# Merged attention of a decoder program: gathers of two batches as plain rows, operand copies part by part, and a new order of VectorE's work

## The chip, the cores and the metric

The program runs on one NeuronCore of a Trainium2 chip. The metric is device time in microseconds (us), from the start of the one launch to its end; lower is better.

## The reference, cut to what matters

The program is a decoder of two layers over 8 batches of 512 tokens, 256 features, in float32. The change touches one stage, `mix_heads`, which finishes the first layer and computes the first two thirds of the second:

```python
# end of layer 0: four expert rows are added to each token
y = y.at[tok].add(out)
# layer 1, a recurrence over time with one decay for each feature, then a 256x256 product
h = h * A + x_t ;  out = einsum('sbd,do->bso', hs, BC)
# layer 1, attention of 16 heads of 16 features: values, keys from the context, queries from x
energy = einsum('nqhd,nkhd->nhqk', q, k) ;  masked where mask == 0
attention = softmax(energy / sqrt(256), axis=3)
out = einsum('nhql,nlhd->nqhd', attention, v) @ Wo.T + bo
# each result is added to x, and each input is layernorm(x)
```

## The kernel before, in words

The tensor `x` lies in SBUF (128 partitions, 32 tiles of 256 features; a batch is 4 tiles). Ahead of this stage the experts' rows were written to DRAM, and `place` holds for each token the numbers of its four rows. A batch passes through three jobs in `mix_heads`:

1. **Gather.** GpSimd issues 16 indirect DMAs (4 tiles, 4 rows of each token), which read rows of `outputs` and add them in flight to `x` (`gathers`, L905). VectorE then takes the statistics (`gathered_sums`, L1292), a chain of tiny operations makes mean and variance (L1305 to L1315), ScalarE the root (L1210), VectorE the reciprocal (`root_of`, L1321).
2. **Recurrence** (`combine`): VectorE normalizes (`rec_norm`, L1329), TensorE transposes (item `rtp`, L1070), VectorE scans (L1337), TensorE multiplies (item `rout`, L1076), VectorE adds to `x` (L1341), then statistics and the chain again (`added_sums`, `norm_all`).
3. **Attention.** Five `prep` items: context transposed (0), normalized x transposed (1), keys (2), queries (3), values (4). Keys and queries are split into three bf16 parts so that bf16 matmuls keep float32's precision: ScalarE writes part 0 (L1166), VectorE the residue (`residue`, L1251), ScalarE part 1 (L1174), GpSimd part 2 (`third_part`, L912). SP stores each part to DRAM (`store_part`, L839) and copies the parts back as stacks, six copies of keys and six of queries for each of the four head groups (`stacks`, L846). On the stacks TensorE computes the energies twice: queries by keys in PSUM `wide` (`first_energies`, L1008), whose row maxima VectorE takes (`maxima`, L1256); and keys by queries in PSUM `slim` with the negated maxima as extra rows (`second_energies`, L1019), which ScalarE turns into `prob` (L1190). The maxima get there through GpSimd (`split_max`, L927 to L933), a TensorE transpose (`rows`, L1039), a VectorE copy (L1262) and a GpSimd DMA (`max_rows`, L939). `values` (L1031) multiplies `prob` with the values; ScalarE copies the result out, TensorE transposes it (`turn`, L1046), VectorE divides (L1269, L1272). Three `fin` items apply the output matrix (L1055, L1061), and VectorE adds to `x` (L1281).

The work is written out by hand, in place of a scheduler. A batch is 4 groups (g) of 8 steps (n); each step is two tiles of second energies and one item of first energies, the latter 12 steps ahead of their use. Tables say at which (g, n) other items stand: `PREP_AT`, `REST_AT` (residue), `PART1_AT`, `FIN_AT`, `REC_AT`, `NORM_AT`, `ADDED_AT`, `SUMS_AT`, `CHAIN_AT`, `ROOT_AT`, `TURN_AT` = 4, `ROWS_AT` = 5. In batch b the attention of b runs, with the preps of b+1, the end of b-1, the recurrence of b+2 and the gather of b+3. The list `BEFORE` is what runs ahead of batch 0: batches 0 and 1 are gathered and mixed there, and batch 0 prepared.

All items of `wide` share two PSUM buffers in turn: an item on TensorE waits until the item two before it in the list of TensorE's order has been read out (`wide_freed`). `slim` has three buffers. Every engine runs its own list strictly in order.

## Time and profile before

| | |
|---|---|
| time, median of 3 runs | 2812.26 us (2808.93 to 2823.7) |
| the profiled execution | 2824.53 us; its span 2822.8 us, 1.7 us lie around it |
| `mix_heads` in the span | from 1061 to about 1785 us |
| batches 1 to 4 in it | about 79 us each |

The profiled execution is 12.3 us above the median and 0.8 us above the slowest of the three runs. Times in the trace count from the span's start. In a row, "[x <-engine tile line]" is the engine's idle time just before the instruction and what ended it; PEld is TensorE's weight load, SPq and POOLq are queues.

### The profile page before, as it was taken

The numbers are of one execution on the slowest core, as the hardware profiler recorded it, in microseconds if no ns is written. First come the engines' busy times: TensorE is split into PE (matmuls) and PEld (weight loads), VectorE is DVE, ScalarE is ACT, GpSimd is POOL, SyncE is SP. The second block draws the span as 40 slices with busy tenths as digits, with TensorE's granted clock in tenths as the row PEclk, the third lists the DMA queues.
The fourth block names the chain that finished last, engine by engine and source line by source line (L and its number), as shares of the span: only waits on it lengthen the run. The fifth ranks groups of instructions, "written<-read, shape, count | busy, mean of one in ns | idle before, by whom it ended". The sixth has DMA issues, their size and how long they took to land. (4 is left out here: it accounts for less than half of the span.)

```text
span 2822.8 us, 40193 instructions
## 1 busy us (share of the span) xinstructions
PE 2320.4 (82%) x12094; PEld 1621.0 (57%) x12095; DVE 1255.2 (44%) x2608; ACT 830.4 (29%) x1871; POOL 884.9 (31%) x1110
## 2 busy tenths in 40 slices
PE   4888685455599983578888889699989999999998
PEld 2444573223377772223333333365569999999997
DVE  4444215552144442567767767258712222222222
ACT  1111110111044441255556666322211221221221
POOL 1000000047600007455535311022225445455443
PEclk9999765778699995689999999899999999999999
DMA  8300110063355546444434310220017777777775
GB/s 282 133 0 0 34 41 16 0 247 116 111 156 156 157 146 101 96 104 98 105 96 99 77 60 27 85 97 30 16 59 236 243 255 237 245 253 236 244 254 161
DMA packets 203554, 360.75 MB, mean 128 GB/s; under 512 B 29302, under 2 KB 182367, under 8 KB 195272
## 3 DMA queue, kind: packets, MB, share of 16 engines
q1 hardware_dynamic: 160456, 299.94, 31.1%
q0 software_dynamic: 43008, 59.70, 10.8%
q8 instruction: 46, 0.75, 0.1%
q14 instruction: 44, 0.36, 0.0%
HBM read 261.83 MB, written 97.13 MB: 127 GB/s over the span
## 5 line engine op out<-in xcount | busy, mean ns | idle before, releaser
L2449 PE MATMUL me_hp<-me_xgT,me_w 128*128 128x160 f32 x3072 | 440.7, 301 | 0.6 <-DVE me_xgT L2491 0.6
L2449 PEld LDWEIGHTS me_hp<-me_xgT,me_w 128*128 128x128 f32 x3072 | 425.1, 191 | 1.5 <-DVE me_xgT L2491 0.7
L1256 DVE TENSOR_REDUCE hd_nmax<-hd_wide 128x2 f32<-128x1024 f32 x256 | 307.8, 1219 | 120.1 <-PE hd_wide L1008 119.5
L1190 ACT ACTIVATE hd_prob<-hd_slim 128x512 f32<-128x512 f32 x512 | 276.3, 601 | 202.6 <-PE hd_slim L1019 201.8
L2505 DVE TENSOR_TENSOR me_hid<-me_act_out,me_hp 128x160 f32<-128x160 f32 x384 | 123.4, 321 | 372.0 <-ACT me_act_out L2477 372.0
L2458 PE MATMUL me_op<-me_hid,me_w 128*128 128x160 f32 x1536 | 236.0, 304 | 0.0
L1019 PE MATMUL hd_slim<-hd_q_stack,hd_k_stack 100*128 100x512 bf16 x512 | 199.0, 392 | 38.9 <-ACT hd_prob L1190 27.5
L1008 PE MATMUL hd_wide<-hd_k_stack,hd_q_stack 97*128 97x512 bf16 x512 | 201.4, 398 | 26.4 <-DVE hd_rest L1251 14.9
L2477 ACT ACTIVATE me_act_out<-me_hp 128x160 f32<-128x160 f32 x384 | 116.4, 303 | 347.6 <-PE me_hp L2449 347.6
L2458 PEld LDWEIGHTS me_op<-me_hid,me_w 128*128 128x128 f32 x1536 | 213.8, 190 | 2.6
L905 POOL DMA_INDIRECT all_x<-outputs,rt_place x128 | 200.6, 1568 | 42.0 <-issue 36.5
L2149 PE MATMUL me_r_hp<-me_r_xnT,me_r_sw 128*128 128x512 f32 x384 | 169.1, 597 | 0.0
L1881 PE MATMUL mr_e_hp<-mr_w,mr_e_xtT 128*128 x640 | 167.7, 385 | 0.8 <-issue 0.8
L1019 PEld LDWEIGHTS hd_slim<-hd_q_stack,hd_k_stack 100*128 100x128 bf16 x512 | 50.0, 99 | 196.3 <-ACT hd_prob L1190 81.2
L1031 PE MATMUL hd_pv<-hd_prob,hd_v 128*32 128x512 f32 x1024 | 139.2, 616 | 3.9 <-ACT hd_oT L1154 3.6
L1733 POOL DMA_INDIRECT places<-mr_s_xn,mr_s_now x128 | 124.6, 974 | 55.2 <-issue 33.2
L2107 POOL TENSOR_TENSOR me_r_hid<-me_r_act_out,me_r_up_out 128x512 f32<-128x512 f32 x48 | 64.4, 1342 | 217.5 <-ACT me_r_up_out L2205 217.5
L2395 POOL DMA_INDIRECT out_x<-me_oa,me_then_a x64 | 104.0, 1625 | 69.5 <-issue 35.8
L2149 PEld LDWEIGHTS me_r_hp<-me_r_xnT,me_r_sw 128*128 128x128 f32 x384 | 73.1, 192 | 85.4 <-issue 85.0
L1937 DVE TENSOR_TENSOR mr_e_hid<-mr_e_act_out,mr_e_hp 128x128 f32<-128x128 f32 x160 | 46.2, 289 | 165.0 <-ACT mr_e_act_out L1913 165.0
L1881 PEld LDWEIGHTS mr_e_hp<-mr_w,mr_e_xtT 128*128 128x128 f32 x640 | 110.3, 193 | 10.4 <-issue 1.6
L2479 ACT ACTIVATE me_oT<-me_op 128x320 f32<-128x320 f32 x64 | 28.0, 437 | 242.1 <-PE me_op L2458 242.1
(373 smaller groups left out, 3674.3 us busy)
## 6 DMA issues: line engine op xcount, KB each, us to landing
me_w<-in_L_ffn_w_exp SPq DMA_DIRECT2D x64, 2304.0 KB, 9.0
places<-z_zero SPq DMA_DIRECT2D x23, 1008.0 KB, 11.0
mr_e_xt<-places SPq DMA_DIRECT2D x160, 144.0 KB, 2.2
outputs<-mr_e_y SPq DMA_DIRECT2D x160, 128.0 KB, 1.7
part_rows<-hd_parts SPq DMA_DIRECT2D x48, 256.0 KB, 2.3
hd_k_stack<-part_rows SPq DMA_DIRECT2D x192, 64.0 KB, 2.4
hd_q_stack<-part_rows SPq DMA_DIRECT2D x192, 64.0 KB, 2.7
mr_w<-in_L_ffn_w_in SPq DMA_DIRECT2D x4, 2048.0 KB, 18.3
```

The lines of the kernel that those rows point to most:

```text
L905: nc.gpsimd.indirect_dma_start(out=x[:, r * TB + j, :], out_offset=None, in_=outputs[:, :], in_offset=bass.IndirectOffsetOnAxis(ap=place[: ...
L1008: last = nc.tensor.matmul(wide[:, at, j, :], q_stack[0:FIRST_ROWS, bt.slot, h, qc * P:(qc + 1) * P], k_stack[0:FIRST_ROWS, bt.slot, h, :], ...
L1019: nc.tensor.matmul(slim[:, slim_slot(bt, item), :], k_stack[:, bt.slot, h, kc * P:(kc + 1) * P], q_stack[:, bt.slot, h, :], start=True, st ...
L1031: last = nc.tensor.matmul(pv[32 * j:32 * j + 32, :], v[:, slot, kc, head(g, j), :], prob[:, kc * GH + j, :], start=(kc == 0), stop=(kc == ...
L1190: nc.scalar.activation(prob[:, u, :], slim[:, slim_slot(bt, item), :], ACT.Exp, scale=D ** -0.5)\
L1256: nc.vector.tensor_reduce(nmax[:, g % 2, n // 2, c:c + 2], wide[:, at], AX.X, ALU.max, negate=True)\
L1733: nc.gpsimd.indirect_dma_start(out=places[:, :], out_offset=bass.IndirectOffsetOnAxis(ap=now[:, j, n:n + 1], axis=0), in_=xn[:, j, :], in_ ...
L1881: last = nc.tensor.matmul(hp[:, v, 0:2 * F], xtT[:, v, c, :], w1[:, bass.ds(e, 1), c, :].rearrange("p a n -> p (a n)"), start=(c == 0), st ...
L2149: last = nc.tensor.matmul(hp[:, u % 2, half, :], sw1[:, c, at:at + P], xnT[:, c, b * S:(b + 1) * S], start=(c == 0), stop=(c == DC - 1))
L2449: last = nc.tensor.matmul(hp[:, f % 3, half * CAP:(half + 1) * CAP], w1[:, sl, c, cols], xgT[:, sl, c, :], start=(c == 0), stop=(c == DC - 1))
L2458: last = nc.tensor.matmul(op[:, c, 0:CAP], w2[:, sl, f, c * P:(c + 1) * P], hid[:, sl, f, :], start=(f == 0), stop=(f == FC - 1))
L2505: nc.vector.tensor_tensor(hid[:, sl, f, :], act_out[:, f % 2, :], hp[:, f % 3, 0:CAP], ALU.mult).then_inc(h_free, 1)
```

## The change

- **Plain gathers for batches 0 and 1.** The 32 indirect DMAs (`gathered_rows`) write rows into tiles of `prob`, which is not yet in use, tile by tile, and add nothing; VectorE adds the four rows and x (`add_rows`: per tile four additions of 128x256 and the statistics). The second batch's gathers move ahead of GpSimd's `third_part(0, 0)`. Three memsets go from GpSimd to VectorE.
- **The list before batch 0.** The recurrence of batch 1 moves behind the first eight energies; `rows(0,0,0)` moves behind its transposes.
- **Stacks part by part.** SP copies all key stacks as soon as the key parts are stored, then the queries' copies of parts 0 and 1, then those of part 2.
- **Split by half.** ScalarE's part 0 and VectorE's residue work on two halves of 512 columns.
- **The tables.** Item `prep` 1 moves from step 1 to 3, `prep` 3 from 4 to 6, the queries' residue from (0,5) to (0,7); GpSimd's part 2 of the queries and the bias move one group later; the recurrence moves two to six steps later, the sums of gathered rows one step, the root of the variance into ScalarE's step (3,7) and VectorE's next batch.
- **VectorE's order in a step.** `turn` stands ahead of the maximum of its step, `rows` right behind it; `normed` stands behind the maximum of step 2 and no longer ahead of the batch.

```diff
-        PREP_AT = (0, 1, 2, 4, 6)
-        REST_AT, PART1_AT = (3, 5), (4, 6)
+        PREP_AT = {0: 0, 2: 2, 3: 1, 4: 4, 6: 3}
+        REST_AT, PART1_AT = ((0, 3), (0, 7)), ((0, 4), (1, 0))
...
-        REC_AT = {(1, 3): ("rtp", 2, 0), (1, 5): ("rtp", 2, 1), (1, 7): ("rout", 2, 0), (2, 3): ("rout", 2, 1)}
-        NORM_AT, ADDED_AT = ((1, 0), (1, 2)), ((2, 0), (2, 5))
-        SUMS_AT, CHAIN_AT, ROOT_AT = ((3, 3), (3, 4)), ((3, 5), (3, 6)), (3, 6)
+        REC_AT = {(1, 5): ("rtp", 2, 0), (1, 7): ("rtp", 2, 1), (2, 3): ("rout", 2, 0), (2, 5): ("rout", 2, 1)}
+        NORM_AT, ADDED_AT = ((1, 1), (1, 3)), ((2, 6), (2, 7))
+        SUMS_AT, CHAIN_AT, ROOT_AT = ((3, 4), (3, 5)), ((3, 6), (3, 7)), (3, 7)
+        ROOTED_AT, NORMED_AT, THIRD_AT = 1, 2, (0, 6)
 
         BEFORE = [("prep", 0, n) for n in (0, 2, 4)] + [("rtp", 0, 0), ("rtp", 0, 1), ("rout", 0, 0), ("rout", 0, 1)]\
-            + [("prep", 0, n) for n in (1, 3)] + [("rtp", 1, 0), ("rtp", 1, 1), ("rout", 1, 0), ("rout", 1, 1)]\
-            + [("energy", 0, n // NSTEP, n % NSTEP) for n in range(NSTEP + LEAD)]
+            + [("prep", 0, n) for n in (1, 3)] + [("energy", 0, 0, n) for n in range(NSTEP)]\
+            + [("rtp", 1, 0), ("rtp", 1, 1), ("rout", 1, 0), ("rout", 1, 1)] + [("energy", 0, 1, n) for n in range(LEAD)]
...
-                    for a in range(2):
-                        sp.wait_ge(part0_ready, b * 2 + a + 1)
-                        store_part(a, 0)
-                        sp.wait_ge(part1_ready, b * 2 + a + 1)
-                        store_part(a, 1)
-                        sp.wait_ge(part2_ready, b * 2 + a + 1)
-                        store_part(a, 2)
-                    sp.wait_ge(stored, (b + 1) * 6 * 16)
+                    for part in range(3):
+                        part_stored(b, 0, part)
+                    sp.wait_ge(stored, b * 96 + 48)
                     for g in range(NG):
-                        stacks(b, g)
+                        stacks(b, g, 0, range(NPAIR))
+                    for part in range(2):
+                        part_stored(b, 1, part)
+                    sp.wait_ge(stored, b * 96 + 80)
+                    stacks(b, 0, 1, range(NPAIR - 1))
+                    part_stored(b, 1, 2)
+                    for g in range(1, NG):
+                        stacks(b, g, 1, range(NPAIR - 1))
+                    sp.wait_ge(stored, b * 96 + 96)
+                    for g in range(NG):
+                        stacks(b, g, 1, range(NPAIR - 1, NPAIR))
...
+                def gathered_rows(r):
+
+                    for j in range(TB):
+                        wait(pool, gathered[j], r * TOP * 16)
+                        for n in range(TOP):
+                            nc.gpsimd.indirect_dma_start(out=row(r, j, n), out_offset=None, in_=outputs[:, :],
+                                                         in_offset=bass.IndirectOffsetOnAxis(ap=place[:, r * TB + j, n:n + 1], axis=0))\
+                                .then_inc(gathered[j], 16)
...
-                gathers(0, 0, ALL)
+                gathered_rows(0)
+                pool.wait_ge(zeroed, 3)
+                pool.wait_ge(ones_loaded, 32)
+                pool.wait_ge(mask_stored, 16)
+                pool.sem_inc(passed, 1)
+                gathered_rows(1)
                 pool.wait_ge(loaded, 8 * 16)
                 third_part(0, 0)
-                gathers(1, 0, ALL)
                 third_part(0, 1)
...
-                        if g == 0 and b < B - 1:
-                            third_part(b + 1, 0)
-                            third_part(b + 1, 1)
-                        if g == 1 and b < B - 1:
+                        if g < 2 and b < B - 1:
+                            third_part(b + 1, g)
+                        if g == NG - 1 and b < B - 1:
                             add_bias(b + 1)
                         if bt.gathers and g < NG - 1:
-                            gathers(b + 3, (0, 4, 10)[g], (4, 10, ALL)[g])
+                            gathers(b + 3, (0, 5, 10)[g], (5, 10, ALL)[g])
...
+                    for c in range(DC):
+                        dve.wait_ge(part0_ready, (b * 2 + a) * DC + c + 1)
+                        nc.vector.tensor_tensor(rest[:, a, c, :], wide[:, at, c, :], parts[:, a, 0, c, :], ALU.subtract)\
+                            .then_inc(rest_ready, 1)
...
+                def add_rows(r):
+
+                    for j in range(TB):
+                        t, at = r * TB + j, (r * TB + j) * TOP
+                        dve.wait_ge(gathered[j], (r + 1) * (16 * TOP))
+                        for n in (0, 2):
+                            nc.vector.tensor_tensor(row(r, j, n), row(r, j, n), row(r, j, n + 1), ALU.add).then_inc(taken, 1)
+                        dve.wait_ge(taken, at + 2)
+                        nc.vector.tensor_tensor(row(r, j, 0), row(r, j, 0), row(r, j, 2), ALU.add).then_inc(taken, 1)
+                        dve.wait_ge(taken, at + 3)
+                        nc.vector.tensor_tensor(x[:, t, :], x[:, t, :], row(r, j, 0), ALU.add).then_inc(taken, 1)
+                        dve.wait_ge(taken, at + 4)
+                        sums(t, 1)
...
                         for n in range(NSTEP):
+                            if n == TURN_AT and not (bt.first and g == 0):
+                                item = ("turn", 0, g)
+                                turn(bt.b * NG + g, bt.slot if g else 1 - bt.slot, (g - 1) % NG, slim_use(bt, item), slim_slot(bt, item))
                             item = ahead(g, n)
                             if not (bt.last and item[1]):
                                 maxima(item[2], item[3], wide_use(bt, item), wide_slot(bt, item))
```

**Place 1: VectorE ahead of batch 0.** The list of VectorE from the first normalization for attention (L1236, and L1262 after) on. Before:

```order
L1251 TENSOR_TENSOR hd_rest<-hd_wide,hd_parts 128x1024
L1292 BN_STATS all_stats<-all_x 128x6 x4
...
L1329 TENSOR_SCALAR hd_xn<-all_x,all_mean,all_rstd 128x256 x4
L1337 SCALAR_TENSOR_TENSOR hd_xT<-hd_decay,hd_wide 128x512 x2
L1341 TENSOR_TENSOR all_x<-all_x,hd_wide 128x512 x2
L1292 BN_STATS all_stats<-all_x 128x6 x4
...
L1256 TENSOR_REDUCE hd_nmax<-hd_wide 128x2 x12
L1262 COPY hd_nrows<-hd_slim 48x128
```

And with the change, from the same residue:

```order
L1280 TENSOR_TENSOR hd_rest<-hd_wide,hd_parts 128x512 x2
L1286 TENSOR_REDUCE hd_nmax<-hd_wide 128x2 x8
L1330 TENSOR_TENSOR hd_prob<-hd_prob 128x256 x2
L1332 TENSOR_TENSOR hd_prob<-hd_prob 128x256
L1334 TENSOR_TENSOR all_x<-all_x,hd_prob 128x256
L1322 BN_STATS all_stats<-all_x 128x6
...
L1381 SCALAR_TENSOR_TENSOR hd_xT<-hd_decay,hd_wide 128x512 x2
L1292 COPY hd_nrows<-hd_slim 48x128
L1385 TENSOR_TENSOR all_x<-all_x,hd_wide 128x512 x2
```

Eight maxima now stand between the queries' residue and all work on batch 1; four more come behind it.

**Place 2: VectorE in batch 6, groups 0 and 1.** Before, from the normalization for batch 7 (L1236) on; L1256 is a maximum, L1269 and L1272 the `turn`, L1281 the second item of `fin`:

```order
L1236 TENSOR_SCALAR hd_xn<-all_x,all_mean,all_rstd 128x256 x4
L1256 TENSOR_REDUCE hd_nmax<-hd_wide 128x2 x4
L1251 TENSOR_TENSOR hd_rest<-hd_wide,hd_parts 128x1024
L1256 TENSOR_REDUCE hd_nmax<-hd_wide 128x2
L1269 RECIPROCAL hd_rsum<-hd_slim 128x16
L1272 TENSOR_TENSOR hd_o<-hd_slim,hd_rsum 128x4x64
L1256 TENSOR_REDUCE hd_nmax<-hd_wide 128x2
L1251 TENSOR_TENSOR hd_rest<-hd_wide,hd_parts 128x1024
L1262 COPY hd_nrows<-hd_slim 48x128
L1256 TENSOR_REDUCE hd_nmax<-hd_wide 128x2 x7
L1269 RECIPROCAL hd_rsum<-hd_slim 128x16
L1272 TENSOR_TENSOR hd_o<-hd_slim,hd_rsum 128x4x64
```

With the change:

```order
L1286 TENSOR_REDUCE hd_nmax<-hd_wide 128x2
L1262 TENSOR_SCALAR hd_xn<-all_x,all_mean,all_rstd 128x256 x4
L1286 TENSOR_REDUCE hd_nmax<-hd_wide 128x2
L1280 TENSOR_TENSOR hd_rest<-hd_wide,hd_parts 128x512 x2
L1299 RECIPROCAL hd_rsum<-hd_slim 128x16
L1302 TENSOR_TENSOR hd_o<-hd_slim,hd_rsum 128x4x64
L1286 TENSOR_REDUCE hd_nmax<-hd_wide 128x2 x2
L1292 COPY hd_nrows<-hd_slim 48x128
L1286 TENSOR_REDUCE hd_nmax<-hd_wide 128x2 x2
L1280 TENSOR_TENSOR hd_rest<-hd_wide,hd_parts 128x512 x2
L1286 TENSOR_REDUCE hd_nmax<-hd_wide 128x2 x4
L1299 RECIPROCAL hd_rsum<-hd_slim 128x16
```

Five maxima stood ahead of group 0's `turn` and now four do; the fifth follows it.

**Place 3: TensorE at step 4 of group 1, with the change** (L1032 is a first energy, L1043 a second, L1085 the item of `fin`, L1070 the `turn`, L1063 the `rows`):

```order
L1032 MATMUL hd_wide<-hd_k_stack,hd_q_stack 128x512
L1085 MATMUL hd_wide<-hd_wo,hd_oT 128x256 x4
L1070 MATMUL hd_slim<-all_ident,hd_oT 128x128 x4
L1043 MATMUL hd_slim<-hd_q_stack,hd_k_stack 128x512
L1032 MATMUL hd_wide<-hd_k_stack,hd_q_stack 128x512
L1043 MATMUL hd_slim<-hd_q_stack,hd_k_stack 128x512
L1032 MATMUL hd_wide<-hd_k_stack,hd_q_stack 128x512
L1063 MATMUL hd_slim<-all_ident_bf,hd_nparts 128x128
```

This order is that of before, with other line numbers: on TensorE the `turn` still stands behind the `fin` or `prep` item of its step.

## Rows read from the trace of the kernel before

**Rows 1.** Windows: busy time of each engine, granted clock (1.00 is full), by stretch.
```profile
1061.00:1168.20 107.20, 41.06 (x114) 22.67 (x115) 46.74 (x93) 9.22 (x12) 72.95 (x58) 0.60 0.60 113
1261.60:1340.00 78.40, 67.84 (x364) 29.09 (x364) 56.19 (x80) 46.28 (x79) 39.04 (x46) 0.98 0.42 96
```
**Rows 2.** Waits of PE, from 1261.6 to 1735 us: total, times, longest.
```profile
PE hd_slim L1039 <- DVE hd_o L1272: 15.7, 13, 2.5
PE hd_wide L1008 <- DVE hd_rest L1251: 12.7, 12, 1.2
...
PE hd_wide L1070 <- DVE hd_xn L1329: 5.6, 5, 1.2
```
**Rows 3.** Timeline, start and duration: the gathers of batch 0 and their statistics.
```profile
1063.42 1.63 POOL L905 DMA_INDIRECT all_x<-outputs,rt_place  x1 [0.28 <-POOL hd_zero L897]
...
1077.45 1.55 POOL L905 DMA_INDIRECT all_x<-outputs,rt_place  x1 [3.90 <-DMA all_x<-outputs,rt_place]
...
1095.99 1.55 POOL L905 DMA_INDIRECT all_x<-outputs,rt_place  x1 [0.30 <-issue]
...
1099.94 0.75 DVE L1292 BATCH_NORM_STATS2 all_stats<-all_x 128x6 f32<-128x256 f32 x2 [2.96 <-DMA all_x<-outputs,rt_place]
```
**Rows 4.** Tiles and lines: issue of plain indirect DMAs, duration ns min/median/max.
```profile
L2009 POOL DMA_INDIRECT me_xa<-token_rows,me_now_a x64: 982/1051/1061, 2079.5 to 2776.6; - x64
L1733 POOL DMA_INDIRECT places<-mr_s_xn,mr_s_now x128: 967/971/1334, 583.6 to 761.0; - x128
```
**Rows 5.** Timeline: two additions of 128x128, then normalization and reciprocal round a recurrence.
```profile
1075.33 0.28 DVE L1242 TENSOR_TENSOR hd_wq<-hd_wq,hd_blocks 128x128 f32<-128x128 f32 x1
1075.54 0.28 DVE L1242 TENSOR_TENSOR hd_wv<-hd_wv,hd_blocks 128x128 f32<-128x128 f32 x1
...
1102.72 1.38 DVE L1329 TENSOR_SCALAR hd_xn<-all_x,all_mean,all_rstd 128x256 f32<-128x256 f32 x4
...
1117.33 0.18 DVE L1321 RECIPROCAL all_rstd<-hd_dev 128x4 f32<-128x4 f32 x1 [0.38 <-ACT hd_dev L1210]
```
**Rows 6.** Timeline: queries' residue, part 2, first stacks, maxima, and the first second energies.
```profile
1126.88 1.23 DVE L1251 TENSOR_TENSOR hd_rest<-hd_wide,hd_parts 128x1024 f32<-128x1024 f32 x1 [7.96 <-ACT hd_parts L1166]
...
1129.28 2.22 POOL L912 TENSOR_TENSOR hd_parts<-hd_rest,hd_parts 128x1024 bf16<-128x1024 f32 x1
...
1133.66 2.93 SPq L846 DMA_DIRECT2D hd_k_stack<-part_rows  x6
...
1136.63 2.81 SPq L846 DMA_DIRECT2D hd_q_stack<-part_rows  x6
...
1151.27 14.12 DVE L1256 TENSOR_REDUCE hd_nmax<-hd_wide 128x2 f32<-128x1024 f32 x12
...
1168.19 0.61 PE L1019 MATMUL hd_slim<-hd_q_stack,hd_k_stack 100*128 100x512 bf16 x1 [3.96 <-DMA hd_q_stack<-hd_nrows]
```
**Rows 7.** Timeline, batch 2, group 1, step 4: energies, output product, turn.
```profile
1372.20 1.89 PE L1061 MATMUL hd_wide<-hd_wo,hd_oT 128*128 128x256 f32 x8
1372.40 1.23 DVE L1256 TENSOR_REDUCE hd_nmax<-hd_wide 128x2 f32<-128x1024 f32 x1 [0.46 <-PE hd_wide L1008]
1373.93 0.60 PE L1046 MATMUL hd_slim<-all_ident,hd_oT 128*128 128x128 f32 x4
...
1374.57 0.26 DVE L1269 RECIPROCAL hd_rsum<-hd_slim 128x16 f32<-128x16 f32 x1 [0.94 <-PE hd_slim L1046]
1374.59 0.38 PE L1008 MATMUL hd_wide<-hd_k_stack,hd_q_stack 97*128 97x512 bf16 x1
...
1374.86 0.42 DVE L1272 TENSOR_TENSOR hd_o<-hd_slim,hd_rsum 128x256 f32<-128x256 f32 x1
```
**Rows 8.** Timeline, batch 2, group 0, steps 3 and 4: maximum, residue, next energy.
```profile
1349.21 1.22 DVE L1256 TENSOR_REDUCE hd_nmax<-hd_wide 128x2 f32<-128x1024 f32 x1 [1.37 <-PE hd_wide L1008]
...
1350.35 1.21 DVE L1251 TENSOR_TENSOR hd_rest<-hd_wide,hd_parts 128x1024 f32<-128x1024 f32 x1
...
1351.62 0.39 PE L1008 MATMUL hd_wide<-hd_k_stack,hd_q_stack 97*128 97x512 bf16 x1 [1.13 <-DVE hd_rest L1251]
```
**Rows 9.** Timeline, batch 2, group 3, steps 3 to 5: statistics, rows, copy of maxima.
```profile
1409.01 0.75 DVE L1292 BATCH_NORM_STATS2 all_stats<-all_x  x2 [1.93 <-DMA all_x<-outputs,rt_place]
...
1411.64 0.10 PEld L1039 LDWEIGHTS hd_slim<-all_ident_bf,hd_nparts 128*128 128x128 bf16 x1 [2.99 <-POOL hd_nparts L933]
...
1414.81 0.20 DVE L1262 COPY hd_nrows<-hd_slim 48x128 bf16<-48x128 bf16 x1
```
**Rows 10.** Timeline: one VectorE addition of 128x4 alone, and one beside GpSimd's part 2.
```profile
1100.73 0.17 DVE L1305 TENSOR_TENSOR all_mean<-all_stats 128x4 f32<-128x4 f32 x1
...
1201.97 4.79 POOL L912 TENSOR_TENSOR hd_parts<-hd_rest,hd_parts 128x1024 bf16<-128x1024 f32 x2
...
1205.67 1.12 DVE L1305 TENSOR_TENSOR all_mean<-all_stats 128x4 f32<-128x4 f32 x1
```

More of the change, by code:

```diff
@@ L1359, in batch @@
                                 maxima(item[2], item[3], wide_use(bt, item), wide_slot(bt, item))
-                            if g == 0 and n in REST_AT and nxt is not None:
-                                item = ("prep", 1, REST_AT.index(n) + 2)
-                                residue(nxt.b, REST_AT.index(n), wide_use(bt, item), wide_slot(bt, item))
-                            if n == TURN_AT and not (bt.first and g == 0):
-                                item = ("turn", 0, g)
-                                turn(bt.b * NG + g, bt.slot if g else 1 - bt.slot, (g - 1) % NG, slim_use(bt, item), slim_slot(bt, item))
                             if n == ROWS_AT and not (bt.last and g == NG - 1):
@@ L1387, in batch @@
                                     gathered_sums(r3, SUMS_AT.index((g, n)))
-                                many = 2 * TB if bt.gathers else TB
                                 if (g, n) == CHAIN_AT[0]:
@@ L1416, in _ @@
                     if item == ("rtp", 1, 0):
-                        for pair in range(2):
-                            gathered_sums(1, pair)
+                        add_rows(1)
                         norm_all(TB, TB, 12, 2)
```

73 lines of the change are left out of this document (41 added, 32 removed).

## The prediction

> **What bounds the kernel now.** I read the windows first. `mix_heads` has two parts that this change touches: an entry of 107.2 us in which TensorE is busy 41 us at a mean granted clock of 0.60, and batches of some 79 us in which it is busy 67.8 of 78.4 us at 0.98 [rows 1]. So the entry is a chain of dependent steps, and a batch is bound by TensorE plus what it waits for. Everything outside the stage is untouched and I take its time as it is.
>
> Then the waits of TensorE over batches 1 to 6 [rows 2]: for VectorE's `turn` (hd_o) 15.7 us in 13 waits, for its residue 12.7 us in 12, for its normalization 5.6 us in 5. All are of VectorE, which is busy 56 of 78 us: it is not full, but its order decides. Last the timeline of the places where something moves.
>
> **Entry, gathers.** GpSimd issues 16 accumulating gathers from 1063.42 to 1097.5 at a pitch of 1.55 + 0.30 us, with a 3.9 us wait for a landing among them; the last statistics end at 1100.7 [rows 3]. The trace shows no plain gather from `outputs`, but one from another tensor at 1.05 us and a plain scatter at 0.97 [rows 4]. I take 1.05 + 0.30 = 1.35 us, and the gathers start at about 1062.2 since the memsets are gone: 16 end at 1083.8, 32 at 1105.4. Now VectorE has to add. An addition of 128x128 has a pitch of 0.21 us and lasts 0.28 [rows 5]; one of 128x256 has 128 more elements at some 1 ns each, so 0.34 and 0.42. A tile has one addition at pitch, three that wait for the one before (0.42 + 0.03 each) and statistics of 0.37 (two in 0.75, [rows 3]): 2.0 us, four tiles 8.2 us. They start behind the keys' residue, at 1087.6, and end at 1095.8, 4.9 us earlier than 1100.7. The queries' residue, which ended at 1128.1 [rows 6], then ends at 1123 (5 us earlier, and a little more for the halves).
>
> **Entry, stacks.** Before, the parts of the queries took until 1131.5, their storing until 1133.7, and the 12 copies of group 0 a further 5.7 us; with 2.5 us to land the first energies could have started at 1141.9 [rows 6]: 13.8 us behind the residue. Now: part 1 at 1124, part 2 at 1126.2, copies of parts 0 and 1 of group 0 from 1126.5 to 1128.9, the store of part 2, then the 15 copies of the other groups at 0.47 us each (7.1 us), and only then the copies of part 2: issued at 1136.8, landed at 1139.3. The key copies (24, 11.4 us) run from 1110.5 to 1121.8, hidden. So the energies of group 0 start at 1139.4, and VectorE has idled for 16 us.
>
> **Entry, order.** Behind that start stand on VectorE eight maxima at 1.18 us (12 took 14.1 us, [rows 6]) = 9.4, `add_rows(1)` 8.2, the chain 2.0, normalization 1.4, then from the end of a normalization (1104.1) to the end of the next reciprocal (1117.5) 13.4 [rows 5], and four maxima 4.7. In all 39.1 us from 1140.1, to 1179.2. TensorE turns to the first second energies two maxima earlier, at about 1177.5; before that was 1168.2 [rows 6], 2.8 us behind the last maximum because the copy of the maxima and its DMA came last, a path that `rows(0,0,0)` now takes early. **Entry: +9 us**. The 16 us of idleness, once filled with batch 1's work, is where it comes from.
>
> **Batches, `turn` first.** At step 4 of group 1 TensorE ends the energy at 1372.2, does the output product until 1374.0, the turn until 1374.5, and starts step 5's energies at 1374.59, because VectorE took the maximum at 1372.40 and left the buffer free; VectorE then waited 0.94 us for the turn and used it until 1375.28 [rows 7]. With `turn` ahead, the maximum starts at 1375.3 and ends at 1376.5. Step 5's energy takes the buffer of step 4's (the item two before, with the product between) and so starts at 1376.55: 1.96 us late. The same holds at group 0, where `prep` 4 (16 matmuls, about 1.95 us) stands in the product's place. Group 0 in batches 1 to 6, group 1 in 1 to 7: 13 x 1.96 = **+25.5**. In groups 2 and 3 nothing stands between energy and turn, step 5 uses another buffer, and it costs nothing.
>
> At (2,5) the item `rout` now follows and takes the buffer of (2,4), whose maximum is behind the turn: TensorE arrives some 1.2 us early, in 6 batches: **+7**.
>
> **Batches, `prep` 1 at step 3.** Before, the energy of step 4 took the buffer of the keys' projection, and TensorE did `values` (1.06 us) between; it still waited 1.13 us for the residue, which came behind the maximum [rows 8]. Now `prep` 1 takes that buffer right behind step 3's energy: the wait grows by `values` and little else, 1.2 us in 7 batches: **+8.4**. Halving the residue gains nothing there, since it waits for VectorE's maximum, not for ScalarE.
>
> **Batches, what is saved.** Of the 15.7 us for `turn`, some 11 stand in group 3, where TensorE at the same moment waits for GpSimd's maxima (2.99 us, [rows 9]); that wait is GpSimd's six gathers, which stay. The other 4.7 go. The queries' residue no longer stands between step 5's maximum and the next: of 6 waits of about 1 us, some 0.7 each, 4 us. The 5.6 us for normalization go, as it gets an earlier place. In group 3 the copy of the maxima came 3.2 us behind `rows` since VectorE waited for the gathered rows [rows 9]; one step later they are there and the copy comes at once, which lets GpSimd start 0.6 us sooner: 3 us in five batches. `prep` 1, the reciprocal and the normalization leave steps 0 and 1: about 0.65 us in 6 batches, 4 us. Sum **-21.3**. Stacks for later batches were ready well ahead and stay so: part 2 of the queries comes at (1,5), its copies land some 14 us later, and seven steps of 2 us and three inserted items lie before their use at (2,4). That cover is some 5 us; without it TensorE would wait for stacks.
>
> **Sum.** 9 + 25.5 + 7 + 8.4 - 21.3 = +28.6. Against the profiled execution of 2824.5: 2853.1. That execution is 12.3 us above the median, so 2841 for the median, 1.0% slower. The measurement can tell about 0.5%, 14 us, from no change.
>
> **A rule weighed.** A VectorE addition of 128x4 takes 0.17 us alone and took 1.12 us beside GpSimd's part 2, ending when that ended [rows 10]. `add_rows` is 16 such two-input additions in each batch, the first lot beside gathers being issued. If these held up each other for the 0.3 us of an addition, 16 of them would put `third_part(0,0)` 5 us later; the key copies would end at 1127 and the first energies start some 3 us later. The Trainium skill (SBUF — State Buffer, the section on the engine side's ports) says that VectorE with two SBUF inputs and a GpSimd operation that reads SBUF take one port pair as an exclusive lock; by that rule, the trace agrees. In the trace the gathers kept 1.55 us whatever VectorE did, so I give the sum nothing for it.
>
> **Rivals.**
> *The order pays (faster).* TensorE's waits on VectorE in a batch are 8 us of its 78 (the four groups took 21.2, 21.8, 15.1 and 20.3 us). If the maximum of step 4 is not what holds step 5, because TensorE gets there later than in rows 7, the +25.5 vanishes; if half of the 8 us went, that is -27 in 6.5 batches, with the entry 2824.5 - 18, for the median 2794. For it: VectorE's waits are many and small. Against: rows 7 have the three times beside each other. It decides at 0.5 us: under that at step 5 of groups 0 and 1, this rival holds. Chance 0.18.
> *Entry late, batches even.* Losses by `turn` and gains at the batch boundary balance: +9, 2821 for the median. For it: a step later elsewhere may hide half of each loss. Chance 0.20.
> *GpSimd is the late one.* If a plain gather costs the 1.86 us of an accumulating one, 32 end at 1121.7 and part 2 of the keys at 1124; key copies until 1138, the queries' until 1153, so the first energies come 14 us later, plus the blocking above, 3: +46, 2858. Against: two plain forms at 1.05 and 0.97 [rows 4]. Chance 0.09.
> *The forecast*, 0.53, with its own range 2826 to 2855: it takes 1.3 to 2.3 us for each late maximum and 5 to 12 us for the entry.
>
> **Numbers.** 2841. The range leaves out half of the first rival and some of the third: 2797 to 2862. Faster by over 0.5% (under 2798) 0.18, within 0.20, slower (over 2826) 0.62.
>
> **What would show it.** The first second energies near 1177; VectorE idle for 16 us before the first maximum; plain gathers near 1.05 us. In batches 1 to 6 a TensorE wait of about 2 us for the maximum at step 5 of groups 0 and 1, and one of over 2 us for the residue ahead of `prep` 1; the waits for hd_o nearly gone; a batch of 81 to 83 us. I am wrong if TensorE reaches step 5 late anyway, if the first energies start much before 1139, or if `rows` in group 3 no longer waits for GpSimd.

## The result, and the profile after

The changed kernel takes 2875.5 us (median of 4 runs, 2866.2 to 2880.2), the kernel before 2815.0 (4 runs): the ratio is 1.0208, 95% interval 1.0169 to 1.0248. That is 60 us at the median. Between the two profiled executions, both of which start the stage near 1061 us, it is 55.7 us (spans 2878.5 and 2822.8): 59.3 us within the stage, less 4.1 behind its last `rows` (1057.4 us before, 1053.3 after). Forecast were 2841 us and a range up to 2862: the sign was right, the size about half.

The windows of the kernel after, first the entry and two batches, then everything between the first `rows` (L1063) at step 5 of batch 0 and the last of batch 7. The columns, as in [rows 1], are the length, the busy time and instructions of TensorE, its weight load, VectorE, ScalarE and GpSimd, the granted clock, the share of the DMA engines and GB/s:

```profile
1061.62:1178.47 116.85, 39.85 (x114) 22.41 (x114) 55.97 (x125) 9.34 (x14) 53.40 (x55) 0.59 0.41 104
1299.30:1384.57 85.27, 71.28 (x365) 30.47 (x364) 57.09 (x82) 46.87 (x82) 39.18 (x46) 0.94 0.39 88
1475.57:1560.92 85.35, 71.16 (x366) 30.03 (x364) 56.19 (x82) 46.95 (x82) 39.11 (x46) 0.94 0.39 88
1197.68:1825.19 627.51, 509.82 (x2624) 209.42 (x2622) 408.44 (x573) 341.24 (x597) 238.52 (x310) 0.93 0.33 76
```

and the last of these for the kernel before:

```profile
1183.99:1765.38 581.39, 486.87 (x2635) 203.60 (x2634) 403.77 (x560) 339.36 (x584) 237.77 (x310) 0.97 0.35 83
```

These two long rows are the main reading. TensorE does the same work in both but for one item at the edge: in batch 0 the window after has the queries' projection (4 matmuls) where before it has that of the values (16), each about 2 us long. Yet it is busy 509.8 us against 486.9. So of the 46.1 us that the batches lost, 23.2 are idle time (117.7 against 94.5, the length less the busy time) and 22.9 are matmuls that took longer. The clock explains them. The stretches of the batches at the 1.2 GHz level, added up, are in the kernel before

```profile
sum 37.55, PE 21.10; mean PE 3.52
```

and after

```profile
sum 85.33, PE 66.83; mean PE 4.18
```

TensorE was busy for 21.1 us at the lower level before and for 66.8 after. Half of the difference is 22.9 us, and the busy time at the full clock plus half of that at the lower is 476.3 us before and 476.4 after. Each of the 16 stretches at the lower level after begins during a stop of TensorE of 1.2 to 3.2 us (the first: 19.5), or within 2 us of its end; not every such stop is followed by one. The forecast had 19.6 us for the batches, all of it waits.

The entry, as a timeline (this answers [rows 3, 6]):

```profile
1064.11 0.96 POOL L926 DMA_INDIRECT hd_prob<-outputs,rt_place  x1 [0.30 <-issue]
...
1139.14 1.44 PE L1032 MATMUL hd_wide<-hd_k_stack,hd_q_stack 97*128 97x512 bf16 x3 [19.82 <-issue]
...
1140.19 9.42 DVE L1286 TENSOR_REDUCE hd_nmax<-hd_wide 128x2 f32<-128x1024 f32 x8 [18.91 <-PE hd_wide L1032]
...
1178.47 0.63 PE L1043 MATMUL hd_slim<-hd_q_stack,hd_k_stack 100*128 100x512 bf16 x1
```

First energies at 1139.1 (forecast 1139.4), VectorE idle 18.9 us before its first maximum (forecast 16), first second energies at 1178.5 (forecast 1179 at the end of the maxima, 1177.5 for TensorE).

TensorE's waits in batches 1 to 6, which answer [rows 2] (total, times, longest):

```profile
PE hd_wide L1032 <- DVE hd_nmax L1286: 22.9, 14, 3.2
PE hd_wide L1011 <- DVE hd_rest L1280: 12.6, 5, 2.6
PE hd_wide L1100 <- DVE hd_nmax L1286: 7.6, 10, 1.1
...
PE hd_slim L1063 <- POOL hd_nparts L954: 4.9, 4, 1.2
```

The wait for hd_o is gone from the head of the list; the wait for a maximum has come. The timeline of the boundary from batch 3 to batch 4 (answers [rows 7, 8]) shows both at work:

```profile
1537.16 0.38 PE L1043 MATMUL hd_slim<-hd_q_stack,hd_k_stack 100*128 100x512 bf16 x1
...
1539.42 0.90 PE L1011 MATMUL hd_wide<-all_ident,hd_cx 128*128 128x128 f32 x3 [1.67 <-DVE hd_nmax L1286]
...
1541.18 0.63 PE L1043 MATMUL hd_slim<-hd_q_stack,hd_k_stack 100*128 100x512 bf16 x1
...
1551.39 1.09 PE L1011 MATMUL hd_wide<-all_ident,hd_xn 128*128 128x128 f32 x8 [2.51 <-DVE hd_rest L1280]
...
1558.64 0.42 DVE L1302 TENSOR_TENSOR hd_o<-hd_slim,hd_rsum 128x256 f32<-128x256 f32 x1
...
1558.98 1.21 DVE L1286 TENSOR_REDUCE hd_nmax<-hd_wide 128x2 f32<-128x1024 f32 x1
...
1560.25 0.39 PE L1032 MATMUL hd_wide<-hd_k_stack,hd_q_stack 97*128 97x512 bf16 x1 [1.72 <-DVE hd_nmax L1286]
```

`prep` 1 waits 2.51 us for the residue, and so at all its seven places (2.51 to 2.59; the first lies ahead of the first `rows` at step 5); step 5 waits 1.72 us for the maximum behind `turn`, at 13 places. And the same matmul of 512 columns lasts 0.38 us before TensorE has stood for 1.67 us at 1539.4 and 0.63 from about 1541 on: between the two, at 1538.8, the granted clock went from 2.4 to 1.2 GHz.

### The profile page after: what moved, and what is told of

Read it like the earlier page. It is cut to its first block and busy times, and to the rows that moved or that the text cites. A ratio compares the mean times of both kernels' runs of the same rounds, so it can differ in the third digit from the quotient of the medians.

```text
span 2878.5 us, 40278 instructions
## 1 busy us (share of the span) xinstructions
PE 2341.0 (81%) x12094; PEld 1623.9 (56%) x12095; DVE 1271.3 (44%) x2659; ACT 832.4 (29%) x1887; POOL 866.7 (30%) x1107
## 3 DMA queue, kind: packets, MB, share of 16 engines
q0 software_dynamic: 39936, 59.70, 10.1%
## 5 line engine op out<-in xcount | busy, mean ns | idle before, releaser
L1286 DVE TENSOR_REDUCE hd_nmax<-hd_wide 128x2 f32<-128x1024 f32 x256 | 305.4, 1217 | 116.9 <-PE hd_wide L1032 113.0
L1032 PE MATMUL hd_wide<-hd_k_stack,hd_q_stack 97*128 97x512 bf16 x512 | 205.1, 406 | 84.4 <-DVE hd_nmax L1286 32.0
L1043 PE MATMUL hd_slim<-hd_q_stack,hd_k_stack 100*128 100x512 bf16 x512 | 202.4, 398 | 8.7 <-DMA hd_q_stack<-hd_nrows 5.0
L917 POOL DMA_INDIRECT all_x<-outputs,rt_place x96 | 150.5, 1567 | 27.8 <-issue 27.6
L1055 PE MATMUL hd_pv<-hd_prob,hd_v 128*32 128x512 f32 x1024 | 146.8, 647 | 5.0 <-ACT hd_oT L1179 4.7
L1043 PEld LDWEIGHTS hd_slim<-hd_q_stack,hd_k_stack 100*128 100x128 bf16 x512 | 50.5, 100 | 172.3 <-issue 69.8
L1032 PEld LDWEIGHTS hd_wide<-hd_k_stack,hd_q_stack 97*128 97x128 bf16 x512 | 50.9, 101 | 151.2 <-DVE hd_nmax L1286 55.4
L1980 DVE TENSOR_TENSOR mr_e_hid<-mr_e_act_out,mr_e_hp 128x128 f32<-128x128 f32 x160 | 46.1, 288 | 165.2 <-ACT mr_e_act_out L1956 165.2
```

What stands on the lines that cost most here:

```text
L917: nc.gpsimd.indirect_dma_start(out=x[:, r * TB + j, :], out_offset=None, in_=outputs[:, :], in_offset=bass.IndirectOffsetOnAxis(ap=place[: ...
L1032: last = nc.tensor.matmul(wide[:, at, j, :], q_stack[0:FIRST_ROWS, bt.slot, h, qc * P:(qc + 1) * P], k_stack[0:FIRST_ROWS, bt.slot, h, :], ...
L1043: nc.tensor.matmul(slim[:, slim_slot(bt, item), :], k_stack[:, bt.slot, h, kc * P:(kc + 1) * P], q_stack[:, bt.slot, h, :], start=True, st ...
L1055: last = nc.tensor.matmul(pv[32 * j:32 * j + 32, :], v[:, slot, kc, head(g, j), :], prob[:, kc * GH + j, :], start=(kc == 0), stop=(kc == ...
L1286: nc.vector.tensor_reduce(nmax[:, g % 2, n // 2, c:c + 2], wide[:, at], AX.X, ALU.max, negate=True)\
```

## The experiments

All 18 kernels are compared by the stage's own marks, since the stage `mix_heads` starts at 1048 to 1064 us in one execution or another, with nothing changed ahead of it. "Entry" is from the start of the stage (its first memset, L887 or L905) to the first second energies, "batches" the stretch of the long rows above, "busy" and "idle" TensorE's within it, "stage" from the start of the stage to the last `rows`. The ratio is to the kernel before.

Each row but the ratio is one execution, and executions of the same code differ. e7 has the code of the kernel before in the batches, e6 that of e5: they agree within 1 us in busy time and within 2 in idle time. e4 has the code of the changed kernel there, and is busy 7.4 us less and idle 3.7 more. The entries of e6, e9, e10 and e11, again one code, spread over 1.6 us, e12 and e13 differ by 3.1, and e14 comes 3.8 behind the changed kernel. So steps from the changed kernel of less than some 8 us of busy time, and entries that differ by less than 4 us, show nothing by themselves.

| kernel | ratio (95%) | entry | batches | busy | idle | stage |
|---|---|---|---|---|---|---|
| before | | 107.1 | 581.4 | 486.9 | 94.5 | 704.3 |
| changed | 1.0208 (1.0169-1.0248) | 116.9 | 627.5 | 509.8 | 117.7 | 763.6 |
| e1_var | 1.0216 (1.0171-1.0261) | 116.9 | 630.7 | 513.8 | 116.9 | 766.8 |
| e2_turn | 1.0114 (1.0081-1.0148) | 117.1 | 595.5 | 500.3 | 95.2 | 731.5 |
| e3_prep1 | 1.0162 (1.0110-1.0215) | 117.0 | 615.9 | 500.3 | 115.6 | 749.0 |
| e4_entry | 1.0164 (1.0131-1.0197) | 104.4 | 623.8 | 502.4 | 121.4 | 746.7 |
| e5_turn_prep1 | 1.0070 (1.0045-1.0096) | 116.8 | 587.5 | 499.8 | 87.7 | 720.2 |
| e6_turn_prep1_entry | 1.0004 (0.9984-1.0024) | 104.3 | 587.5 | 500.2 | 87.3 | 707.5 |
| e7_plain | 0.9991 (0.9972-1.0011) | 108.2 | 580.6 | 487.9 | 92.7 | 704.3 |
| e8_turn_first | 1.0129 (1.0088-1.0169) | 107.0 | 609.3 | 500.3 | 109.0 | 732.3 |
| e9_bias | 0.9960 (0.9935-0.9985) | 105.0 | 580.4 | 493.4 | 87.1 | 701.0 |
| e10_root | 1.0021 (0.9998-1.0044) | 105.2 | 587.9 | 494.1 | 93.8 | 708.7 |
| e11_both | 0.9969 (0.9947-0.9992) | 103.6 | 575.5 | 488.0 | 87.4 | 694.9 |
| e12_prep | 0.9963 (0.9939-0.9987) | 102.1 | 576.1 | 491.3 | 84.7 | 693.6 |
| e13_third | 0.9955 (0.9936-0.9975) | 105.1 | 575.6 | 485.7 | 89.9 | 696.3 |
| e14_bias_changed | 1.0136 (1.0101-1.0170) | 120.6 | 617.5 | 505.7 | 111.7 | 757.3 |
| e15_bias_before | 1.0048 (1.0022-1.0073) | 107.8 | 592.8 | 493.7 | 99.1 | 716.1 |
| e16_stacks | 0.9935 (0.9911-0.9959) | 103.3 | 564.1 | 485.2 | 78.9 | 683.1 |

### e1: the variance a step earlier

```diff
-        ... CHAIN_AT, ROOT_AT = ((3, 4), (3, 5)), ((3, 6), (3, 7)), (3, 7)
+        ... CHAIN_AT, ROOT_AT = ((3, 4), (3, 5)), ((3, 5), (3, 6)), (3, 7)
```

> The changed kernel with one table entry different: VectorE ends the variance chain at steps (3,5) and (3,6) instead of (3,6) and (3,7), while ScalarE's root stays at (3,7). Theory A (ScalarE is held, and that is on the path): ScalarE's wait for hd_var, 13.2 us in 5 waits between 1299 and 1790 us, goes, the stretch from `rows` of group 3 to `rows` of group 0 gets 2 to 2.5 us shorter in six batches, and the span falls by 12 to 15 us from 2878.5 to about 2865. Theory B (it is hidden, because TensorE at that moment waits for VectorE's maximum anyway): 0 to 4 us, 2875 to 2878.

Nothing gained (stage +3.2, busy +4.0, idle -0.8). ScalarE's wait for hd_var over the batches only fell from 31.5 to 27.0 us, and behind it TensorE still stood for the residue. Theory A fell.

### e2, e3, e5: `turn` and `prep` 1 undone, alone and together

```diff
# e2: the four lines of maxima stand ahead of those of turn again
# e3:
-        PREP_AT = {0: 0, 2: 2, 3: 1, 4: 4, 6: 3}
+        PREP_AT = {0: 0, 1: 1, 2: 2, 4: 4, 6: 3}
-        ROOTED_AT, NORMED_AT, THIRD_AT = 1, 2, (0, 6)
+        ROOTED_AT, NORMED_AT, THIRD_AT = 0, 0, (0, 6)
```

> The changed kernel with VectorE's `turn` put back behind the maximum of its step; nothing else differs. Theory A (the forecast's term): the waits of 1.7 us at step 5 of groups 0 and 1 go, the span falls by 22 to 26 us to about 2854. Theory B (the order pays: something else is late at that place): 0 to 5 us. Theory C (each wait of TensorE also lowers its granted clock for a while): the fall is 30 to 35 us, to about 2846, and TensorE's busy time from `rows` of group 3 to `rows` of group 0 falls too.

> The changed kernel with `prep` 1 back at step 1, and the reciprocal and the normalization at step 0 behind its maximum (they stood ahead of it before the change). Theory A (the forecast's terms: +8.4 us for the move, -4 us for clearing steps 0 and 1): the span falls by 4 to 8 us, to about 2872. Theory C (the wait of 2.5 us ahead of `prep` 1 and the lower granted clock behind it are worth 4 us in each of seven batches): it falls by 20 to 28 us, to about 2854.

> The changed kernel with both edits of the two earlier runs undone: `turn` behind its maximum and `prep` 1 at step 1. Theory W (waits alone; each costs its own length): the stretch from `rows` of group 3 to `rows` of group 0, 26.0 us with `turn` undone alone, falls by the 2.5 us of the wait ahead of `prep` 1 to about 23.5, and the span to about 2828. Theory C (the waits also bring a stretch at half the granted clock, which goes only when they are all short): it falls to 21.5 to 22.5 us at a granted clock of 0.92 or more, and the span to 2814 to 2820.

e2: the stage is 32.1 us shorter; idle -22.5, as much as 13 waits of 1.72, and busy -9.6. That is Theory C by its size, though e4 is busy 7.4 us less with no such edit; the clean test of C is e8. e3 alone: -14.6, between A and C, of which 3.0 lie ahead of the batches; idle only -2.1 and busy -9.5. The 13 waits at step 5 stay at 1.72 us; the waits for the residue fall by 7.9 us, but 2.8 us come for ScalarE's copy of the context (hd_cT) and some 3 us elsewhere. With both undone the idle time falls by 7.5 against e2, near the forecast's 8.4 for `prep` 1. But the stretch from `rows` of group 3 to that of group 0 stayed at 24.5 to 25.2 us at a granted clock of 0.86 (27.4 at the loop's end): neither theory had it, something else was still late there.

### e4, e6, e7: the entry

```diff
-            + [("prep", 0, n) for n in (1, 3)] + [("energy", 0, 0, n) for n in range(NSTEP)]\
-            + [("rtp", 1, 0), ("rtp", 1, 1), ("rout", 1, 0), ("rout", 1, 1)] + [("energy", 0, 1, n) for n in range(LEAD)]
+            + [("prep", 0, n) for n in (1, 3)] + [("rtp", 1, 0), ("rtp", 1, 1), ("rout", 1, 0), ("rout", 1, 1)]\
+            + [("energy", 0, n // NSTEP, n % NSTEP) for n in range(NSTEP + LEAD)]
# e6: e5 with this, and rows(0, 0, 0) behind ("energy", 0, 1, 1)
# e7: the kernel before with gathered_rows and add_rows for batches 0 and 1 in place of gathers and sums
```

> The changed kernel with the list ahead of batch 0 in its old order (recurrence of batch 1, then twelve energies, then `rows`); gathers, additions and stacks stay as changed. Theory A (the forecast's term, the 16 us of idleness are filled again): the first energies still start at 1139 to 1140 us, the twelve maxima end near 1155 and the first second energies start at about 1157 to 1159, 20 us earlier than 1178.5; the span falls to about 2859. Theory B (the additions of batch 1 hold the queries' residue or the stacks, which come as late as what they save): the first second energies stay within 5 us of 1178.

> The kernel of the run before this one, and also the list ahead of batch 0 in its old order, with `rows` of group 0 two energies behind the eighth and not at the end of the list. The old order gave 11.4 us at the first second energies (1167.1 against 1178.5), which the earlier `rows` raise to 13 to 14, since the wait of 3.8 us for the maxima's copy goes: first second energies at 1164 to 1165. Theory W: span about 2814. Theory C: 2801 to 2807, faster than before by 0.5% or more.

> The kernel before with the plain gathers and the additions on VectorE for batches 0 and 1, and nothing else of the change. The forecast's term: the last statistics of batch 0 end 5 us earlier, so the first residue of the queries too; then the additions of batch 1 cost VectorE 6.7 us more than its statistics did, ahead of the twelve maxima. Theory A: gain and cost leave 2 to 5 us, span 2818 to 2821. Theory B (the additions of batch 1 stand on the path and the gain does not): slower by up to 3 us, 2823 to 2826.

The old order gave 12.5 us at the entry (104.4 against 116.9): the term of +9 holds. The 20 us that I expected did not come: VectorE is with batch 1's additions and recurrence until 1150.3, not until the first energies at 1139, and the twelve maxima (14.1 us) stand behind that. Of the 7.5 us that are missing 3 are `add_rows(1)`, which took 11.2 us and not 8.2 beside GpSimd's part 2 (last section). The earlier `rows` of e6 gave nothing to see: its maxima started 2.3 us later than those of e4 (89.9 and 87.6 us behind the stage's start), in code that is the same up to there, and the entry came out equal. Its span, 2822.1 us, is above both theories. e7 shows the plain gathers alone: entry +1.1, stage the same, ratio 0.9991, between A and B. They neither cost nor bring anything in the old order.

### e8: `turn` first, in the kernel before

> The kernel before with `turn` ahead of the maximum of its step, and nothing else of the change. Theory W (the forecast's term alone, 13 waits of 1.7 to 2 us, less the 4.7 us of waits for hd_o that go): 18 to 22 us slower, span about 2843. Theory C (with a lower granted clock behind the waits): 28 to 33 us slower, about 2854. Rival (the order pays or does nothing on the old tables): within 5 us of 2823.

The long row of this kernel:

```profile
1175.21:1784.54 609.33, 500.31 (x2635) 205.51 (x2634) 401.95 (x560) 341.87 (x584) 238.08 (x310) 0.94 0.34 79
```

Stage +28.0: idle +14.5, busy +13.4. Theory C, with one edit to the kernel before, whose busy time e7 repeats within 1.0. TensorE's waits for hd_o went altogether (18.6 us over the batches), and 11.9 us of waits for GpSimd's maxima came: the forecast's "some 11 stand in group 3" and stay. "The order pays" is dead.

### e9, e10, e11, e14, e15: GpSimd's bias and the root

```diff
# e9 (on e6), e14 (on the changed kernel)
-                        if g == NG - 1 and b < B - 1:
+                        if g == 1 and b < B - 1:
                             add_bias(b + 1)
# e10 (on e6): chain at (3, 5), (3, 6), root at (3, 6); e11: both
# e15: g == 1 made g == NG - 1 in the kernel before, nothing else
```

> The kernel with `turn`, `prep` 1 and the list ahead of batch 0 undone (batches 587.5 us from the first to the last `rows` of the eight batches, TensorE busy 500.2 and idle 87.3 of them; before 581.4, 486.9 and 94.5), and GpSimd's bias back from group 3 to group 1. Theory P (GpSimd's additions hold up VectorE's chain of tiny operations, 0.64 us each against 0.17, so the variance, the root and ScalarE's exponentials are late and the clock falls): the chain's operations take 0.17 to 0.20 us again, ScalarE's wait for hd_var shrinks from 2.3 to about 1 us, the stretch from `rows` of group 3 to that of group 0 falls from 24.5 to 22.5 us or less, batches 573 to 578 us. Theory R (the place of the root alone decides): the chain is quicker, but the stretch stays at 24 to 24.5 and the batches at 585 or more.

> The same kernel with the bias left in group 3, and instead the chain and the root one step earlier: (3,5), (3,6) and the root at (3,6), as before the change. Theory R: ScalarE is free for the exponentials of step 7 as before, the stretch from `rows` of group 3 to that of group 0 falls to 22.5 us or less, batches 573 to 578 us. Theory P: the chain now runs beside the bias all the same (or waits for it), the stretch stays at 23.5 to 24.5, batches 583 to 588 us.

> Both of the two edits before. Both theories: the stretch at 22 us or less with the granted clock at 0.92 to 1.00, TensorE busy about 487 us in the batches and idle about 85, batches 570 to 575 us, the first second energies 104.3 us behind the stage's start (before 107.1), so that the stage is 8 to 12 us shorter than before and the ratio 0.996 to 0.997. If the clock has a cause of its own that no wait explains, TensorE stays busy for 495 us or more.

> The changed kernel with nothing undone but GpSimd's bias, from group 3 back to group 1. Theory P (port): VectorE's chain at 0.17 us an operation, not 0.64; TensorE idle in the batches stays at 115 to 118 us, its busy time falls from 509.8 by 5 to 10 us, the span falls by 6 to 12 us to about 2869. Rival (hidden behind the wait ahead of `prep` 1): within 3 us of 2878.5.

> The kernel before with nothing changed but GpSimd's bias, from group 1 to group 3. Theory P: VectorE's chain of tiny operations at (3,5) takes 0.64 us each, ScalarE's root and the exponentials behind it come 1 to 2 us later, the stretch from `rows` of group 3 to that of group 0 grows from 22.3 to 23.5 to 24.5 us, batches 588 to 594 us instead of 581.4, the kernel 0.2 to 0.4% slower. Rival (VectorE and ScalarE have the time): batches within 2 us of 581.4.

The timeline of the kernel after, group 3 of batch 1: four additions of the bias, and VectorE's chain beside them:

```profile
1359.92 2.79 POOL L939 TENSOR_TENSOR all_x<-all_x,hd_bias 128x256 f32<-128x256 f32 x4
...
1361.43 0.64 DVE L1350 TENSOR_SCALAR all_mean<-all_mean  x1
...
1362.10 0.64 DVE L1351 TENSOR_TENSOR hd_half_diff<-all_stats 128x8 f32 x1
...
1364.81 0.21 ACT L1236 ACTIVATE hd_dev<-hd_var 128x8 f32<-128x8 f32 x1 [2.55 <-DVE hd_var L1359]
```

and of e9, the same operations without the bias beside them:

```profile
1406.98 0.17 DVE L1350 TENSOR_SCALAR all_mean<-all_mean  x1
...
1407.19 0.17 DVE L1351 TENSOR_TENSOR hd_half_diff<-all_stats 128x8 f32 x1
```

0.64 us against 0.17, and 0.64 is near the 0.70 us of one addition (2.79 for four). The Trainium skill (SBUF — State Buffer, the section on the two separate sides) has VectorE and GpSimd take one pair of ports as an exclusive lock, held for a whole instruction, when VectorE's instruction has two SBUF inputs and GpSimd's reads SBUF, or when VectorE's is in a two-port mode. By that rule, the trace agrees. The late variance holds ScalarE at the root (its waits for hd_var are 0.6 to 1.8 us in the batches of the kernel before and 1.1 to 3.2 in e15, but for one of 16.5 in batch 0 in both), its exponentials come late, and in e15 TensorE stands 4.6 us longer and its clock falls. e9: idle the same, busy -6.8 us, batches 580.4, a little above what P gave. e10 alone gained nothing (busy -6.1, idle +6.5; the chain mostly at 0.60 to 0.71 us again, R fell), both together (e11) brought busy to 488.0, as in the kernel before, and the batches to 575.5, near what both theories gave. e15, the bias alone moved in the kernel before, costs 11.4 us in the batches (busy +6.8, idle +4.6) and 0.48% in all: more than P expected. In e15:

```profile
1175.77:1768.57 592.80, 493.72 (x2636) 207.24 (x2634) 412.32 (x560) 339.44 (x584) 237.78 (x310) 0.95 0.35 81
...
1330.33 2.79 POOL L918 TENSOR_TENSOR all_x<-all_x,hd_bias 128x256 f32<-128x256 f32 x4
1330.43 0.68 DVE L1308 SCALAR_TENSOR_TENSOR hd_half_diff<-hd_half_diff 128x8 f32<-128x8 f32 x1
...
1333.39 0.21 ACT L1210 ACTIVATE hd_dev<-hd_var 128x8 f32<-128x8 f32 x1 [3.21 <-DVE hd_var L1315]
```

e14 takes the bias out of the changed kernel: batches -10.0 us (idle -6.0, busy -4.1). Here I had expected no change of the idle time. The ratio fell by 0.0072, about 20 us with some 15 either way.

### e12, e13, e16: the stacks

```diff
# e12 (on e11)
-        PREP_AT = {0: 0, 1: 1, 2: 2, 4: 4, 6: 3}
-        REST_AT, PART1_AT = ((0, 3), (0, 7)), ((0, 4), (1, 0))
+        PREP_AT = {0: 0, 1: 1, 2: 2, 4: 3, 6: 4}
+        REST_AT, PART1_AT = ((0, 3), (0, 5)), ((0, 4), (0, 6))
# e13 (on e12): third_part(b + 1, 0) and third_part(b + 1, 1) both at g == 0
# e16 (on e12)
                     part_stored(b, 1, 2)
-                    for g in range(1, NG):
-                        stacks(b, g, 1, range(NPAIR - 1))
                     sp.wait_ge(stored, b * 96 + 96)
-                    for g in range(NG):
-                        stacks(b, g, 1, range(NPAIR - 1, NPAIR))
+                    stacks(b, 0, 1, range(NPAIR - 1, NPAIR))
+                    for g in range(1, NG):
+                        stacks(b, g, 1, range(NPAIR))
```

> The kernel before this one and also the queries' projection back at step 4, its residue at (0,5) and part 1 at (0,6), as before the change. Theory S (the late stacks of the queries hold TensorE in group 2 of batch 0, 2.4 to 2.9 us and a clock dip): the stretch from `rows` of group 1 to that of group 2 in batch 0 falls from 21.9 to 17.6 to 18.5 us, the others change by less than 1 us. Rival (the stacks are in time either way, and the residue of the queries at (0,5) holds a maximum): no change there, and 0.5 to 1 us more from group 0 to group 1 in each batch, 3 to 6 us slower in all.

> The kernel of the run e12 (everything undone but gathers, stacks, halves and recurrence tables), with GpSimd's part 2 of the queries back right behind that of the keys in group 0. Theory T (the part is made a group late): the parts are stored 17 us earlier, the wait of 2.5 us for the stacks in group 2 of batch 0 goes, and the stretch from `rows` of group 1 to that of group 2 there falls from 21.5 to 17.6 to 18.2 us; batches 570 to 573 us. Rival: that stretch stays above 20 us, because the granted clock there has another reason.

> The kernel of the run e12, with part 2 of the queries left in group 1 of GpSimd, and only SP's order changed: the copies of part 2 for group 0 right behind its storing, ahead of the 15 copies of the other groups. Theory S (those 15 copies, 7 us, stand in the way): the copies for group 0 are issued by 1210.6 instead of about 1214 to 1216 on the scale of e12, the wait of 2.5 us goes or shrinks below 0.5, the stretch falls to 17.6 to 19 us; in the entry the first energies could start up to 7 us earlier but VectorE is busy with batch 1's recurrence, so nothing is gained there. Rival: part 2 itself is late, the wait stays above 2 us.

In e12 the stretch from group 1 to group 2 of batch 0 stayed at 21.5 us (17.6 before): S, as put there, fell (its rival's 3 to 6 us did not come either, the batches took 0.6 more than in e11). Its timeline says why, on SP's queue and TensorE:

```profile
1206.66 0.38 SPq L844 DMA_DIRECT2D part_rows<-hd_parts  x1
...
1207.08 8.97 SPq L859 DMA_DIRECT2D hd_q_stack<-part_rows  x19
...
1218.50 0.38 PE L1032 MATMUL hd_wide<-hd_k_stack,hd_q_stack 97*128 97x512 bf16 x1 [2.54 <-issue]
```

The store of part 2 was issued at 1206.7; of the 19 copies behind it (0.47 us each) the first 15 are those of the other groups, and the one of group 0, which is needed first, comes 16th, near 1214. e16 changes only this order, and Theory S holds: the wait is gone and that stretch becomes 17.5 us, the same stretch of batches 1 to 4 falls to 20.2 (20.3 to 23.5 in e12, 20.4 to 20.5 before), idle time by 5.8 and busy time by 6.1. e13 gets 18.9 us there by storing the part sooner, but 21.3 to 22.8 in batches 1 to 4, between its two theories; why was not followed up. e16 beats the kernel before and the changed one: 2797.2 us, ratio 0.9935 (0.9911 to 0.9959). Over the whole time it is not told apart from e12 (2799.6 us, 0.9963, the intervals overlap); its 12 us in the batches are one execution of each.

## Why the prediction was wrong, point by point

- **Entry +9: right, with some luck.** +9.8 at the first second energies, with plain gathers at 0.95 us (forecast 1.05), the idle VectorE and the eight maxima as forecast. That the first energies hit to 0.3 us is luck: the queries' residue ended at 1121.3 (forecast 1123), and the energies came 17.9 us behind it (forecast 16.4). Another 3.4 us came until the first `rows` at step 5, 2.5 of them the wait ahead of `prep` 1.
- **`turn` first +25.5: right, a little too large.** 13 waits of 1.72 us and not 1.96, 22.4 us; e2 gave 22.5 of idle time, e8 showed that some 12 of the hd_o waits come back as waits for GpSimd.
- **`rout` at (2,5) +7: too large.** The waits there were up to 1.1 us, and 8.2 us for both `rout` items over the batches against 4.3 before: 3.9 is new, since the item waited 0.4 us already.
- **`prep` 1 +8.4: right.** 2.51 against 1.13 us in seven batches is 9.7; e5 against e2 gave 7.5.
- **Saved -21.3: about 11 came out.** The idle time rose by 23.2 where the first three terms measured about 34.5 within the batches. The waits for hd_o and for the normalization did go, and the stretch from group 2 to group 3 became 1.0 us shorter. Part of what was not saved is at step 0: TensorE waits there 1.6 to 1.8 us for a maximum (1539.4 in the rows above), 8.6 us in all, and where the variance is earlier it waits 4.1 (e1) or 2.9 (e14). An estimate from single executions: the moved bias (idle 4.6 us in e15, 6.0 in e14) and the wait for stacks (2.4) account for 7 to 8 of the missing 10. That the idle time of the batches came near the forecast, 23.2 for 19.6, is therefore partly luck: the priced costs were too large by some 6 us, and two costs were left out.
- **The sum took each wait at its own length: the step that failed.** The batches' waits were forecast at +19.6 us and came to +23.2. But in [rows 1] a batch ran at 0.98, and I took the clock as given. After the longer stops the granted clock fell to the 1.2 GHz level and matmuls of 0.38 us took 0.63: 22.9 us, as much again as the waits (15.5 us in e4, with the same code in the batches). That added waits bring it is shown by single edits to the kernel before: e8 (idle +14.5, busy +13.4) and e15 (+4.6 and +6.8). Between the profiled executions the forecast was 27.1 us short (28.6 for 55.7): the clock is 22.9 of them, idle time in the batches 3.6, the entry up to the first `rows` at step 5 4.2 and the stage's start 0.5, less the 4.1 behind the stage.
- **Two edits that I priced at nothing.** GpSimd's bias in group 3, beside VectorE's chain (e9, e14, e15: 7 to 11 us). And SP's order, where I had named the cover ("some 5 us; without it TensorE would wait for stacks") and put it on seven steps of 2 us: in batch 0 the copies of group 0 stood behind 15 others, and the cover was gone (2.4 us in the changed kernel and a lower clock, 5.6 us from group 1 to group 2; e16 gives them back).
- **The rule weighed.** I looked for the port at the entry, beside the gathers, and rightly gave it nothing there: the gathers kept 0.95 us, two of the 32 took 1.14 and 1.20. It acted at the moved bias, where I did not look.
- **Rivals.** The order does not pay (e8). GpSimd's gathers are not late (0.95 us). Entry late and batches even is refuted by 46 us.

What stays open: how the 22.9 us divide among the waits. Each undone edit gives back a different share, and they do not add up: e2 and e3 gave 9.6 and 9.5 us of busy time, both together 10.1. e4 gave 7.4 with nothing undone in the batches, so this single execution of the changed kernel may stand above others of it; the division can't be read from one execution of each. e10's busy time fell by 6.1 us while its idle time rose by 6.5, which was not followed up either.

## What to carry to other kernels

Compare TensorE's busy time over the same matmuls before and after: where it differs, part of the loss can be clock, which the granted clock of the same stretches confirms. Added waits then cost more than their length; here, idle and busy time together, 2.0 times in the changed kernel, 1.9 in e8 and 1.6 in e4. Repeat a kernel before reading a difference of a few us from one execution. When an edit moves a GpSimd operation that "has time", look at which small VectorE operations stand beside it, and at who waits for those. When DMA copies are regrouped, follow the first consumer and keep its copies at the head of the queue.
